# The one-hot rows' product with the tile's number: VectorE or GpSimd

## What is computed

```python
x = x + 0.5 * _L0_ffn_ref(_layernorm(x), ...)     # FFN with 4-bit quantisation of its inputs
x = x + _L0_attn_ref(_layernorm(x), ...)          # causal attention with rotary positions
x = x + 0.5 * _L0_ffn_ref(_layernorm(x), ...)
x = x + 0.5 * _L1_ffn_ref(_layernorm(x), ...)     # experts: 8, each token goes to its best 2
x = x + _L1_attn_ref(_layernorm(x), ...)          # windowed attention
x = x + 0.5 * _L1_ffn_ref(_layernorm(x), ...)     # experts
```

```python
logits = xf @ router_w.T
topk_scores, topk_ids = jax.lax.top_k(jax.nn.softmax(logits, axis=-1), TOP_K)
topk_scores = topk_scores / topk_scores.sum(-1, keepdims=True)
# out = sum over the 8 experts of  weight * (silu(xf @ wg) * (xf @ wu)) @ wd
```

## Time and profile before

| | us |
|---|---|
| three runs, median | 1661.95 |
| lowest and highest | 1661.44, 1663.56 |
| profiled execution, its own time | 1660.28 |
| its span, first to last instruction | 1658.5 |

### The profile page before, as it was taken

The page is one execution under the profiler, slowest core; times in us unless marked ns, Lnnn a source line. Parts: engine busy times, 40 slices in busy tenths (PEclk is TensorE's granted clock), DMA queues, the critical chain, the costliest instruction groups (busy, mean ns, idle before and its releaser), DMA issues.

```text
span 1658.5 us, 32029 instructions
## 1 busy us (share of the span) xinstructions
PE 1241.3 (75%) x10217; PEld 813.6 (49%) x10218; DVE 1004.2 (61%) x2010; ACT 686.3 (41%) x1292; POOL 659.8 (40%) x867
## 2 busy tenths in 40 slices
PE   0566648999974566539999972799998646999992
PEld 0344435666653444526666650455555344666661
DVE  5677658999946777472322326889998464323223
ACT  0222214655553222224344434366766523444445
POOL 2333412221202444015555641467676203556561
PEclk9877758999997887559999995799999857999996
DMA  8000022322200000101111123343333100111115
GB/s 253 0 0 0 0 38 49 54 58 58 44 18 0 0 0 1 51 7 36 40 40 40 40 73 88 53 78 59 72 69 60 32 21 22 41 39 41 38 41 166
DMA packets 161953, 75.50 MB, mean 46 GB/s; under 512 B 126539, under 2 KB 153940, under 8 KB 161876
## 3 DMA queue, kind: packets, MB, share of 16 engines
q1 hardware_dynamic: 152404, 55.06, 15.0%
q0 software_dynamic: 9472, 19.42, 4.0%
HBM read 28.69 MB, written 15.86 MB: 27 GB/s over the span
## 4 chain that ended last, share of the span: by engine, by line
PE 56%; DVE 23%; POOL 6%; issue 6%; ACT 4%; DMA 3%; SPq 1%; DVEq 1%; POOLq 0%; ACTq 0%
PE PS L927 15%; PE PS L953 8%; PE PS L593 4%; PE PS L308 4%; PE PS L943 4%; POOL q_mg L141 3%; DVE sg L727 2%; DVE m L727 2%; PE PS L559 2%; PE PS L575 2%; POOL xhq L143 2%; PE PS L512 2%; PE PS L317 1%; PE PS L547 1%; PE PS L888 1%
## 5 line engine op out<-in xcount | busy, mean ns | idle before, releaser
L927 PE MATMUL PS<-wgu,xTs 128*128 x584 | 302.9, 602 | 4.4 <-issue 3.2
L1051 DVE TENSOR_TENSOR pt<-pt,PS 128x512 f32<-128x512 f32 x146 | 100.3, 687 | 295.3 <-PE PS L927 295.3
L652 ACT ACTIVATE pt<-PS 128x768 f32<-128x768 f32 (+1 forms) x256 | 227.5, 917 | 108.0 <-PE PS L575 56.3
L1164 POOL DMA_INDIRECT xs<-rows,src x152 | 147.3, 969 | 190.6 <-DVE src L1045 144.9
L1173 POOL DMA_INDIRECT outs<-ys,dst x144 | 142.0, 986 | 159.8 <-DVE ys L1059 154.3
L989 ACT ACTIVATE pt<-PS 128x512 f32<-128x512 f32 x146 | 87.2, 597 | 234.4 <-PE PS L927 234.4
L141 POOL TENSOR_TENSOR q_mg<-q_xn,q_mg 128x960 f32<-128x960 f32 (+3 forms) x37 | 74.1, 2002 | 274.2 <-DVE q_xn L117 274.2
L953 PEld LDWEIGHTS PS<-wdn,pt 128*128 128x128 f32 x1152 | 139.5, 191 | 55.6 <-issue 55.6
L953 PE MATMUL PS<-wdn,pt 128*128 x1152 | 162.9, 284 | 0.7 <-issue 0.7
L727 DVE TENSOR_REDUCE m<-PS 128x4 f32<-128x1024 f32 x128 | 149.0, 1216 | 10.8 <-PE PS L512 10.3
L512 PE MATMUL PS<-tables 64*128 64x128 bf16 (+2 forms) x1536 | 131.6, 251 | 0.0
(11 more groups left out here) (215 smaller groups left out, 2287.4 us busy)
## 6 DMA issues: line engine op xcount, KB each, us to landing
pt<-outs SPq DMA_DIRECT2D x16, 512.0 KB, 5.0
rows<-qT SPq DMA_DIRECT2D x12, 256.0 KB, 2.6
xs<-rows,src POOLq DMA_INDIRECT x152, 2.5
outs<-ys,dst POOLq DMA_INDIRECT x144, 2.3
wgu<-in_L_ffn_w_gate SPq DMA_DIRECT2D x1, 2048.0 KB
wgu<-in_L_ffn_w_up SPq DMA_DIRECT2D x1, 2048.0 KB
wdn<-in_L_ffn_w_down SPq DMA_DIRECT2D x8, 256.0 KB
qT<-hqT SPq DMA_DIRECT2D x128, 4.0 KB
```

The costliest lines, as they stand in the source:

```text
L652: s.activation(k.pt[:, a % 4, :, 0:w], k.PS[:, self.bank:self.bank + 2, 0:w], ACT.Exp, scale=self.scale).then_inc(self.s_p, 1)
L927: t.matmul(k.PS[:, 1 + 2 * p + w, :], k.xTs[:, p, :], k.wgu[:, w, ds(e, 1), :].squeeze(1), start=True, stop=True).then_inc((self.s_gate_ps ...
L1164: g.indirect_dma_start(k.xs[:, i % RING, :], None, k.rows[:, :], bass.IndirectOffsetOnAxis(ap=k.src[:, i:i + 1], axis=0)).then_inc(self.s_ ...
```

## The change

L1034, the product of eqa and the tile's number, moves from VectorE to GpSimd, with a semaphore of its own, `s_tile`. VectorE's second comparison tells `s_hot` now. GpSimd does the eight products of a layer at the head of its part, ahead of its waits for the lists; each waits for its comparison (`s_eq`) and, from the third on, for the buffer (`s_list_ps`). TensorE waits for `s_tile` too. Shapes, types and buffers are as before.

```diff
@@ tensor
             eng.wait_ge(self.s_hot, g + 1)
             eng.wait_ge(self.s_part, g + 1)
+            eng.wait_ge(self.s_tile, g + 1)
@@ vector, hot
-            hotb, eqa, tiles = (x[:, u, :, :].rearrange("p (r j) c -> p r j c", r=2) for x in (k.hotb, k.eqa, k.hota))
+            hotb, eqa = (x[:, u, :, :].rearrange("p (r j) c -> p r j c", r=2) for x in (k.hotb, k.eqa))
             iota = k.iotab[:, :].unsqueeze(1).unsqueeze(1)
-            tile = k.iotab[:, ds(g * GT + 2, GT)].unsqueeze(1).unsqueeze(3).broadcast_to(n)
             v.tensor_tensor(eqa, iota[:, :, :, 0:NL].broadcast_to(n), k.qab[:, :, at].unsqueeze(3).broadcast_to(n),
                             ALU.is_equal).then_inc(self.s_eq, 1)
             v.tensor_tensor(hotb, iota.broadcast_to([P, 2, GT, P]),
-                            k.qb[:, :, at].unsqueeze(3).broadcast_to([P, 2, GT, P]), ALU.is_equal)
-            eng.wait_ge(self.s_eq, g + 1)
-            v.tensor_tensor(tiles[:, :, :, 0:NL], eqa, tile, ALU.mult).then_inc(self.s_hot, 1)
+                            k.qb[:, :, at].unsqueeze(3).broadcast_to([P, 2, GT, P]), ALU.is_equal).then_inc(self.s_hot, 1)
@@ gpsimd
+        for i in range(NG):
+            n, u = [P, 2, GT, NL], i % 2
+            eqa, tiles = (x[:, u, :, :].rearrange("p (r j) c -> p r j c", r=2) for x in (k.eqa, k.hota))
+            tile = k.iotab[:, ds(i * GT + 2, GT)].unsqueeze(1).unsqueeze(3).broadcast_to(n)
+            eng.wait_ge(self.s_eq, i + 1)
+            if i >= 2:
+                eng.wait_ge(self.s_list_ps, i - 1)
+            g.tensor_tensor(tiles[:, :, :, 0:NL], eqa, tile, ALU.mult).then_inc(self.s_tile, 1)
         eng.wait_ge(k.sem("pad_rows_stored"), 32)
         eng.wait_ge(self.s_stored, 16 * NG)
         eng.wait_ge(self.s_list, 1)
```

More of the change, by code:

```diff
@@ L849, in __init__ @@
         self.s_part = k.sem(name + "_part")
+        self.s_tile = k.sem(name + "_tile")
         self.s_eid = k.sem(name + "_eid")
```

## The result

| | before | after |
|---|---|---|
| median | 1661.95 us | 1666.9 us |
| lowest and highest of 7 runs | 1658.13 to 1663.56 | 1664.04 to 1668.63 |
| profiled execution, span | 1658.5 | 1665.1 |

The ratio is 1.0033, 95% interval 1.002 to 1.0045: slower by a third of a per cent, 5.0 us between the medians (3.3 to 7.5 us by the interval). 1667.4 us was forecast.

A forecast was written before the change was run, and what follows sets the result against it. VectorE was taken as the bound in both expert stages; +0.39, +2.38 and -0.05 us give +2.72 us a stage, +5.4 us for both, so a median of 1667.4 us, range 1662 to 1672 us.

The forecast's parts named there:

- The bound: Both expert stages, first comparison to the copy of the lists: VectorE's own instructions set the end, 22.0 us.
- The exclusion: VectorE comparisons with two SBUF operands and GpSimd's product take turns, hiding only start-up, 0.13 to 0.14 us on GpSimd.
- The price of the product: GpSimd's 608-element product taken as 1.22 us; 1.47 us the upper end, 1.09 if bfloat16 is cheaper, 0.75 the lower end.
- The sum: Each expert stage: a group takes 2.88 us against 2.54; +2.72 us a stage, +5.4 us for both.
- The first product's end: Start of each expert stage: the first product ends at 718.89 instead of 718.50, +0.39 us.
- Seven groups: The remaining groups of each expert stage: 7 x 0.34 = +2.38 us.
- The tail: From the last product's end to the copy of the lists: 1.56 us against 1.61, -0.05 us.
- The shape: Profile after: product about 2.2 us, list comparison about 1.8 in groups 1 to 7, row comparison 1.21, L1149 about 1.8.
- No exclusion: Rival: GpSimd runs beside the comparisons, VectorE's group is 1.84 us, 11.2 us shed in all, 1650.7 us; chance 0.11.
- rival 4: VectorE's next comparison goes ahead of the waiting product: 3.13 us a group, 1670.9 us; chance 0.21 together with rival 3.
- Rivals 2 and 3: 2: exclusion, product 1.09 us or under, chance 0.18; 3: product 1.47 us, 1671.4 us, 0.21 together with rival 4.
- The buffer: Doesn't bind: TensorE is done 1.26 us after a product, before the next comparison into that buffer starts.

The follow-up runs named there:

- e6_act2: Kernel before, with the product of two of each group's four tiles on ScalarE instead of VectorE, GpSimd idle: ratio 0.9978.
- e4_psum_pool: Changed kernel with the small tables qab and qb in PSUM as float32, so each comparison has one SBUF operand: ratio 0.9937, 1649.9 us.
- e1_serial: Changed kernel, but VectorE's row comparison waits until GpSimd's product of the same group is done: ratio 1.0091.
- x_mult: Kernel before plus one extra 608-element product on GpSimd per group, for which no other engine waits: ratio 1.011.
- x_memset: Kernel before plus a GpSimd memset of a 608-element scratch tile per group, which only writes: ratio 1.0001.
- x_copy: Kernel before plus a GpSimd copy of 608 bfloat16 elements per group, reading one SBUF operand: ratio 1.005.
- e8_qab_only: Changed kernel with qab alone in PSUM, so only the list comparison has one SBUF operand: ratio 0.9979.
- e5_psum_dve: Kernel before, product still on VectorE, with qab and qb in PSUM as float32: ratio 0.9995.

## Why the prediction was right, point by point

- **The bound.** VectorE's chain set the stretch before and, with GpSimd's turns in it, after. e6_act2 and e4_psum_pool show that a shorter chain there shortens the kernel by as much, within the intervals: 4.4 us between the medians for 5.1 in the stretches, and 11.2 for 11.2.
- **The exclusion.** It was read from the earlier trace rows, from other instructions of other types. The changed kernel has it at 16 places, and e1_serial, x_mult, x_memset, x_copy and e4_psum_pool show it and its conditions: the second SBUF operand on VectorE, reading on GpSimd.
- **The price of the product.** 1.22 us was taken from the form with a repeating operand in the earlier trace rows; e1_serial has 1.20 us. The 1.47 us of the full operands and the 1.09 us of a cheaper bfloat16 were both wrong. That float32 rows would hold for bfloat16 operands was a choice and no row of before showed it; at 1.09 us the forecast would have been 3.4 us instead of 5.4, so that the number came so close is in part luck; the sign is not.
- **The sum.** A group 2.88 us, measured 2.845 on average. The first product's end +0.39 us, measured +0.36 (2.99 us after the first comparison's start, 2.63 before). Seven groups +2.38, measured +2.14. The tail -0.05, measured -0.05 (739.57 to 741.13). Together +2.72 a layer, measured +2.44. The excess is 0.035 us a group: 0.02 us of it is the product (1.06 us from the row comparison's end to its own, not 1.08), the rest the two handings over.
- **The shape.** Product about 2.2 us (2.12), list comparison about 1.8 (1.79), row comparison 1.21 (1.21), L1148 about 1.8 (1.77): as written.
- **The rivals.** No exclusion (1650.7 us) fell with the change itself; e4_psum_pool, where exclusion is gone, came to 1649.9. That VectorE keeps the turn (rival 4) fell too: there is a product between any two row comparisons. The order stays as rows 6 had it. Rivals 2 and 3 differed in the price alone and fell with the 1.20 us.
- **The buffer.** "It doesn't bind" held for the change, though TensorE is done 1.31 us after a product and not 1.26; e8_qab_only found where it stops holding.

## What to carry to other kernels

Before moving an element-wise step to GpSimd, look in the trace for a place where both engines already work on SBUF, and compare one line's shortest and longest instruction there. If they spread as 277 and 795 ns do, read the ends in order of time, as in the earlier trace rows, to see whether they take turns. If they do, and VectorE is the bound with two SBUF operands in the instructions beside, the move adds GpSimd's working time to VectorE's chain, and pays only if that is less than VectorE's own share. A busy share doesn't tell, since waiting counts as busy. Then see whether the VectorE instruction beside it can take one operand from PSUM, which here turned +0.3% into -0.6%, or whether ScalarE can do the step, which gave -0.2% for half of the product.

## What the runs showed of the hardware that was not expected

- VectorE comparisons of bfloat16 in SBUF with a float32 table in PSUM were as fast as with both operands in SBUF: 0.78 and 1.21 us (e5_psum_dve).
- A GpSimd copy that reads one operand costs VectorE's chain half of what a product does: 0.49 us a group for 608 elements, as much as a two-operand product of 304 elements (0.50 us). A memset of the same size takes 0.60 us and costs the chain nothing (x_memset).
- The turns repeat almost exactly: in both layers of the changed kernel every product ended 1.06 or 1.07 us after the row comparison, and every next list comparison 0.65 us after the product. Of the product's 1.20 us alone (e1_serial), 0.14 us of start-up are hidden each time.
- Two of ScalarE's activations of 152 elements took 0.53 us together, where I had taken 0.72.
